# Decoder layer on one core: the feed-forward's base product in rounded halves, the normed result transposed amid the scores

## The reference

```
x = layernorm(x + mixer(x))                         # state-space mixer, 128 heads
a = softmax(x @ context^T);  x = layernorm(x + a @ context)   # per sequence, 1500 context rows
logits = x @ W_router.T;  w = normalised top 2 of softmax(logits) over 8 experts
h = x @ lora_A (8 experts x 16);  lora = (h * w) @ lora_B * 2
x = layernorm(x + x @ W_base.T + b_base + lora)
```

## Time and profile before

| | value |
|---|---|
| median of three runs | 1457.46 us |
| profiled execution, its own time | 1460.17 us |
| its span, first to last instruction | 1458.4 us |
| TensorE busy | 97% of the span |
| VectorE, ScalarE, GpSimd busy | 68%, 52%, 35% |
| mean granted TensorE clock | 0.991 of 2.4 GHz |
| chain that ended last | TensorE 89%, VectorE 6%, ScalarE 2% |
| context transfers | two of 1,024 KB to a unit, three units to a pair |

### The profile page before, as it was taken

The page is one execution under the profiler, slowest core; times in us unless marked ns, Lnnn a source line. Parts: engine busy times, 40 slices in busy tenths (PEclk is TensorE's granted clock), DMA queues, the critical chain, the costliest instruction groups (busy, mean ns, idle before and its releaser), DMA issues.

```text
span 1458.4 us, 29669 instructions
## 1 busy us (share of the span) xinstructions
PE 1418.3 (97%) x12560; PEld 1160.6 (80%) x12560; DVE 986.8 (68%) x1304; ACT 758.7 (52%) x1022; POOL 505.0 (35%) x374
## 2 busy tenths in 40 slices
PE   6999999999999999999999999999999998999996
PEld 5888989898989888988898889888888854545452
DVE  5784768476847684768476747674767496888764
ACT  6775637563746274637463646364636345543340
POOL 5252425242534153415342534243424221112101
PEclk9999999999999999999999999999999998999998
DMA  5431213121312131213121322131212177566600
GB/s 166 124 106 51 86 44 99 59 86 40 100 55 87 41 99 59 82 41 99 59 83 40 100 59 87 44 99 63 74 52 70 73 277 263 191 256 266 189 29 13
DMA packets 53405, 142.57 MB, mean 98 GB/s; under 512 B 9781, under 2 KB 9909, under 8 KB 47011
## 3 DMA queue, kind: packets, MB, share of 16 engines
q1 hardware_dynamic: 51604, 137.13, 28.9%
q0 software_dynamic: 1600, 3.44, 0.7%
q10 hardware_dynamic: 70, 0.11, 0.0%
HBM read 136.53 MB, written 2.29 MB: 95 GB/s over the span
## 4 chain that ended last, share of the span: by engine, by line
PE 89%; DVE 6%; ACT 2%; issue 1%; POOL 1%; DMA 0%; SPq 0%; DVEq 0%; POOLq 0%; ACTq 0%
PE bank L1231 45%; PE bank L1298 20%; PE bank L1539 6%; PE bank L1454 5%; PE bank L1275 4%; PE bank L1262 4%; PE bank L1511 2%; DVE conv L863 1%; PE bank L1525 1%; DVE keysT L990 1%; PE bank L1507 1%; DVE decay L922 1%; PE bank L1285 1%; PE bank L1519 1%; PE bank L1499 0%
## 5 line engine op out<-in xcount | busy, mean ns | idle before, releaser
L1231 PE MATMUL bank<-h_hi,w_hi 128*128 128x448 f32 x1152 | 337.6, 374 | 2.7 <-DVE conv L863 2.1
L437 POOL TENSOR_TENSOR y_lo<-yg,y_hi 128x896 fp32r<-128x896 f32 x63 | 134.2, 2130 | 582.4 <-ACT y_hi L621 542.4
L1231 PE MATMUL bank<-h_lo,w_hi 128*128 128x448 f32 x1152 | 327.4, 365 | 0.0
L1231 PE MATMUL bank<-h_hi,w_lo 128*128 128x448 f32 x1152 | 326.9, 365 | 0.0
L863 DVE SCALAR_TENSOR_TENSOR conv<-bank,conv_w,conv 128x880 f32<-128x880 f32 (+2 forms) x240 | 268.0, 1117 | 84.9 <-ACT conv L594 79.1
L1231 PEld LDWEIGHTS bank<-h_hi,w_lo 128*128 128x128 f32 x1152 | 216.4, 188 | 17.4
L1231 PEld LDWEIGHTS bank<-h_lo,w_hi 128*128 128x128 f32 x1152 | 216.4, 188 | 17.1
L420 POOL TENSOR_TENSOR w_lo<-w_raw,w_hi 128x512 fp32r<-128x512 f32 x144 | 186.9, 1299 | 109.5 <-ACT w_hi L561 108.1
L1231 PEld LDWEIGHTS bank<-h_hi,w_hi 128*128 128x128 f32 x1152 | 207.9, 188 | 20.7 <-DVE conv L863 2.6
L910 DVE TENSOR_TENSOR hd_dt<-bank,dt_j 128x512 f32<-128x512 f32 x128 | 82.4, 685 | 203.3 <-PE bank L1262 203.0
L1298 PE MATMUL bank<-wo_hi,y_hi 128*128 128x512 f32 x420 | 165.3, 394 | 0.0
(11 more groups left out here) (182 smaller groups left out, 1906.4 us busy)
## 6 DMA issues: line engine op xcount, KB each, us to landing
w_raw<-in_w_in SPq DMA_DIRECT2D x144, 256.0 KB, 2.9
decay<-cs_scratch SPq DMA_DIRECT2D x128, 196.0 KB
ring_a<-in_context SPq DMA_DIRECT2D x24, 1024.0 KB, 7.2
ring_b<-in_context SPq DMA_DIRECT2D x21, 1024.0 KB
wo_raw<-in_w_out SPq DMA_DIRECT2D x64, 256.0 KB, 2.7
ring_b<-in_context SPq DMA_DIRECT2D x3, 896.0 KB
acc<-in_x SPq DMA_DIRECT2D x1, 1792.0 KB, 8.9
out<-z POOLq DMA_DIRECT2D x14, 112.0 KB, 3.9
```

Source lines behind the costliest of these rows:

```text
L437: g_.tensor_tensor(y_lo[:, c % 4, :], yg[:, c % 2, :], y_hi[:, c % 4, :].bitcast(f32), ALU.subtract).then_inc(s["y_low"], 1)
L1231: last = mm(place, w[:, k * P:(k + 1) * P], x[:, k, half * HALF:(half + 1) * HALF], start=(k == 0 and i == 0), stop=(k == KT - 1 and i == 2))
```

## The change

The base product takes three of the four 128-feature blocks in rounded pieces. The weight block is split into a rounded high part `wb_hi` and the rest `wb_lo`, the data into `x2hi` and `x2lo` (type float32r), and three products (high by high, high by low, low by high) take the place of one float32 product. The fourth block stays float32 (`wb_end`). ScalarE makes `wb_hi` once at the end of round 0, GpSimd makes `wb_lo` once in round 1 (in the place of the raw weights); each pair ScalarE makes `x2hi` and VectorE `x2lo`.

The third norm works in place in `x2`, so that `z3` goes; `add_bias` now waits for the transposes of `x2`. `x1p` has two buffers instead of three, and `load_x1` runs one pair ahead instead of two.

The order changes too. `turn_x2(u-1)` stands ahead of block 12 of `score(u)`. `turn_queries` follows `turn_probs` in all rounds. VectorE transposes half 0 of all three units ahead of the three halves 1. In round 0 `last_sum(4..6)` and two sets of statistics come behind `score_max(0)`.

```diff
             def feed_forward(u):
...
                 at_least(pe, s["ffn_read"], u)
-                for k in range(KT):
-                    mm(ffn, x2T[:, k, :], wbT[:, k, :], start=(k == 0), stop=False)
+                mm(ffn, x2T[:, KT - 1, :], wb_end[:], start=True, stop=False)
+                pe.wait_ge(s["x2hi_set"], u + 1)
+                for k in range(KT - 1):
+                    mm(ffn, x2hi[:, k, :], wb_hi[:, k, :], start=False, stop=False)
+                if u == 0:
+                    pe.wait_ge(s["wb_low"], 1)
+                for k in range(KT - 1):
+                    mm(ffn, x2hi[:, k, :], wb_lo[:, k, :], start=False, stop=False)
+                pe.wait_ge(s["x2lo_set"], u + 1)
+                for k in range(KT - 1):
+                    mm(ffn, x2lo[:, k, :], wb_hi[:, k, :], start=False, stop=False)
...
             def score(u):
...
                     if b == 0:
-                        pe.wait_ge(s["kT_set"], 12 * u + 10)
+                        pe.wait_ge(s["kT_set"], 12 * u + 6)
...
+                    if b == 12:
+                        turn_x2(u - 1)
...
             def x2_evac(u):
                 act.wait_ge(s["x2_tr"], u + 1)
-                a(x2T[:], misc.rearrange("p (k t) -> p k t", k=KT), ACT.Copy).then_inc(s["x2_evac"], 1)
+                at_least(act, s["ffn_done"], u)
+                src = misc.rearrange("p (k t) -> p k t", k=KT)
+                a(x2T[:], src, ACT.Copy).then_inc(s["x2_evac"], 1)
+                act.wait_ge(s["x2_evac"], u + 1)
+                a(x2hi[:], x2T[:, 0:KT - 1, :], ACT.Copy).then_inc(s["x2hi_set"], 1)
...
+            def base_low():
+                pool.wait_ge(s["wb_high"], 1)
+                g_.tensor_tensor(wb_lo[:], wb_raw[:], wb_hi[:].bitcast(f32),
+                                 ALU.subtract).then_inc(s["wb_low"], 1)
...
+            def x2_low(u):
+
+                dve.wait_ge(s["x2_evac"], u + 1)
+                dve.wait_ge(s["x2hi_set"], u + 1)
+                at_least(dve, s["ffn_done"], u)
+                v.tensor_tensor(x2lo[:], x2T[:, 0:KT - 1, :], x2hi[:].bitcast(f32),
+                                ALU.subtract).then_inc(s["x2lo_set"], 1)
...
             for u in range(PAIRS + 1):
...
-                if following:
+                if following and u >= 1:
                     keys_part(u + 1, 0, 0)
+                    keys_part(u + 1, 1, 0)
+                if u >= 1:
+                    x2_low(u - 1)
...
                 if following:
-                    keys_part(u + 1, 0, 1)
+                    keys_part(u + 1, 2 if u >= 1 else 0, 0)
...
+                if u == 0:
+                    keys_part(1, 1, 0)
+                    keys_part(1, 2, 0)
+                    for t in range(4, TT):
+                        last_sum(t)
                 if following:
-                    keys_part(u + 1, 1, 0)
+                    keys_part(u + 1, 0, 1)
                     keys_part(u + 1, 1, 1)
...
-                    keys_part(u + 1, 2, 0)
                     keys_part(u + 1, 2, 1)
-                if u + 4 < TT:
-                    norm1_stats(u + 4)
+                if u == 0:
+                    norm1_stats(2)
+                if 0 < u <= TT - 3:
+                    norm1_stats(u + 2)
```

More of the change, by code:

```diff
@@ L144, in layer_kernel @@
         x2T = sb("x2T", [P, KT, P], f32, att)
-        wbT = sb("wbT", [P, KT, DM], f32, att)
+        x2hi = sb("x2hi", [P, KT - 1, P], f32r, att)
+        x2lo = sb("x2lo", [P, KT - 1, P], f32r, att)
+        wb_hi = sb("wb_hi", [P, KT - 1, DM], f32r, att)
+        with ExitStack() as raw:
+            wb_raw = sb("wb_raw", [P, KT - 1, DM], f32, raw)
+        wb_lo = sb("wb_lo", [P, KT - 1, DM], f32r, att)
+        wb_end = sb("wb_end", [P, DM], f32, att)
         waT = sb("waT", [P, KT, P + EXP], f32, att)
@@ L253, in x1_landed @@
         def x1_landed(u):
-            return 16 * sum(x1_pieces(k) for k in range(u % 3, u + 1, 3))
+            return 16 * sum(x1_pieces(k) for k in range(u % 2, u + 1, 2))
         def at_least(eng, semaphore, value):
@@ L739, in queries @@
                 src = turn.rearrange("p (k t) -> p k t", k=KT)
-                for c in blocks:
+                for c in range(4):
                     for row in range(4):
                         last = a(qT[SQ * row:SQ * (row + 1), :, c, :], src[SQ * c:SQ * (c + 1)], ACT.Copy)
-                if 3 in blocks:
-                    last.then_inc(s["q_set"], 1)
+                last.then_inc(s["q_set"], 1)
             def first_queries():
@@ L784, in _ @@
             first_queries()
-            for t in range(1, 4):
-                first_norm(t)
+            first_norm(1)
             for u in range(PAIRS):
@@ L1068, in _ @@
                 last_halves(t)
[L1069 to L1072, removed]
+            last_sum(1)
+            norm1_stats(1)
+            last_sum(2)
+            last_sum(3)
             steps = [1]
@@ L1500, in turn_x2, with score @@
                 last.then_inc(s["x2_tr"], 1)
+            def score(u):
+                pe.wait_ge(s["q_set"], u + 1)
+                pe.wait_ge(s["exps_done"], u)
+                pe.wait_ge(s["pT_evac0"], u)
+                pe.wait_ge(s["pT_evac12"], 2 * u)
+                for b in range(NB):
+                    if b == 0:
+                        pe.wait_ge(s["kT_set"], 12 * u + 6)
+                    elif b == NB // 2:
+                        pe.wait_ge(s["kT_set"], 12 * u + 12)
+                    if b == 12:
+                        turn_x2(u - 1)
+                    last = score_block(b)
+                    if b % 8 == 7:
+                        last.then_inc(s["s_mm"], 1)
             def feed_forward(u):
```

96 lines of the change are left out of this document (39 added, 57 removed).

## The result

The changed kernel takes 1460.21 us (median of 19 runs, 1456.95 to 1464.07) where the kernel before, run beside it, takes 1457.79 us (19 runs, 1456.45 to 1459.38). The ratio is 1.0017, 95% interval 1.0011 to 1.0024: 2.4 us slower. The forecast was 1455.4 with a range to 1460.2, so the time lies just above the range and the sign is the other one. The difference is under the 0.2% that the prediction held to be beyond measuring; with 19 runs of each kernel it stands clear of the noise.

A forecast was written before the change was run, and what follows sets the result against it. TensorE's own instructions were taken to bound the attention rounds. Gains of 3.1, 3.5 and 1.0 us minus losses of 0.2 and 5.3 made 2.1 less: 1457.46 to 1455.4 us, with an 8-in-10 range of 1449.8 to 1460.2.

The forecast's parts named there:

- round 6: Attention round 6: counted like any normal round, 0.58 us gained, with no wait for pair 7's units in the sum.
- round 0: First round: earlier row maximum gains 3.1 us at the softmax; pair 1's x1p rows arriving late cost 0.2.
- round 1: Second round: units behind the feed-forward weights make TensorE wait 2.7 us, plus slow clock; 5.3 us lost, bounds 0 and 8.
- rounds 2 to 5: Normal attention rounds: each gains 0.58 us net and takes 29.1 us, with no softmax wait exposed.
- round 7 and end: Last round: it has no turn_queries and waits 0.69 us for x2T, so it gains 1.0 us.
- Base product and transposes: TensorE in each normal round: 0.4 from the base product plus 0.35 from transposes minus 0.18, net 0.58 us gained.
- the hidden wait for x2T: Between turn_x2's transposes and the router product: the 0.25 us wait and late start go, 0.35 us gained a round.
- the break: Scores interrupted once more by turn_x2's small tiles: costs 0.18 us a round, bounds 0 and 0.5.
- Hiding the softmax: Between scores and turn_probs: 4.0 us of TensorE work covers 3.6 us of softmax; margin shrinks from 2.2 to 0.4 us.
- Rival B: Round 6: third unit lands some 17 us into the scores, about 3 us wait, 2 more to clock; 1460.5 or 1463; chance 0.12.
- rival D: Round 6: the 2.44 us TensorE stop with its slow stretch (4.6 us) goes and no unit wait comes; 1450.8 us; chance 0.08.
- The step from profile to median: Whole kernel: predicted profile 1458.1 us; the earlier profile's 2.7 us above median carried over, so 2.1 is taken off 1457.46.

The follow-up runs named there:

- e3_sums_first: Changed kernel with all seven sums ahead of the first row maximum, so the feed-forward weights load early: 1456.68 us, ratio 0.9998 to the kernel before.
- e5_sums_first_r6_later: Changed kernel with all seven sums ahead of the first maximum and, in round 6 alone, the second and third unit's parts behind the maximum: 1450.86 us, ratio 0.9942.
- e2_units_later: Changed kernel, but in rounds 1 and 6 VectorE takes the row maximum ahead of the second and third unit's parts: 1450.72 us, ratio 0.9954 to the kernel before.
- e11_changed_again: The changed kernel run again unaltered for a second profile: 1461.25 us.
- e9_x1_from_scalar: e2_units_later with pair 1's rows of x1 issued by ScalarE after its first norm, not by GpSimd: 1449.91 us, ratio 0.9947 to the kernel before.
- e10_before_third: The kernel before run again unaltered for a third profile: 1457.99 us.

## Why the prediction was wrong

The step that failed is the one on round 6: the new wait behind the third unit of pair 7 was put at nothing in the sum, and the long stop of one execution was taken for the kernel's own. The runs show 2.85 and 1.95 us of wait with the lower clock behind it, and without it round 6 is 4.8 us shorter (34.59 in e3_sums_first, 29.83 in e5_sums_first_r6_later). Means over the profiles in the table (three of before, two of the changed kernel) against the terms of the sum:

| term | predicted | measured |
|---|---|---|
| round 0 | -2.9 | -2.0 |
| round 1 (its share of 0.6 included) | +4.7 | +5.3 |
| rounds 2 to 5 | -2.3 | -1.8 |
| round 6 | -0.6 | +0.8 |
| round 7 and end | -1.0 | -1.0 |
| sum | -2.1 | +1.3 |

**Base product and transposes: right.** The best round loses 0.72 us where 0.58 was predicted. The halves save 0.50 (0.4 predicted), the hidden wait for x2T and the late starts around it 0.49 (0.35 predicted), the break costs 0.26 (0.18 predicted, within its bounds). Hiding the softmax held with its thin margin: no round from 2 to 5 waits for it. But rounds 2 to 5 gain only 1.8 us together, since not every round is like the best one; round 4, which holds a small stop, takes 30.03 and 30.08 us in the two profiles. The steps costed at nothing or beside other work came near their sizes: x2_low 0.52 us, wb_hi 1.47, wb_lo 3.48.

**Round 1: right in mechanism and near in size.** The forecast had the second unit at 1231 and a wait of 2.7 us; it was 1233 and 2.4 us with TensorE itself 1.9 us later than assumed. In the second profile TensorE starts these scores at 1219.4, as the forecast had it; there the unit comes at 1234.4, and the waits make 5.2 us. So the landing of the unit was put 2 to 3 us too early. That the moved sums caused the wait was shown by e3_sums_first.

**Round 0: mis-sized.** The gain of 3.0 us at turn_probs came as worked out. "x1p of pair 1 may land just after its transposes are due; 0.2 off" was too little: the wait was 1.9 us in the first profile, 0.8 in the second, and 0.8 to 2.8 in the other kernels with the same source of these rows.

**Round 6: the step that failed.** The sum held nothing for it. Rival B named the mechanism, its place and nearly its size (the third unit some 17 us in, a wait of about 3; it came 17.0 us in), but set it aside because "where the old stop of TensorE stays, the new wait lies under it". It did not lie under it. In the first profile the old stop is absent, which was the first half of rival D, and TensorE waits 2.85 us for the copy with the slow clock behind; in the second it has a stop of 0.89 and a wait of 1.95. The other half of the error is the scale: the stop of before was taken at 4.6 us from a single execution (34.60 against 29.69 makes 4.9), while two more show 2.3 and 3.0. Against the mean round 6 of before, 33.07, the changed one is 0.8 us longer, and without the wait it would be 3.7 us shorter (e2_units_later: 29.39).

**The step from profile to median.** "It lies 2.7 us above the median of the runs, and I take the difference to that median" treated those 2.7 us as an overhead that both kernels share. They were mostly the one slow stretch. The profiled time of the changed kernel, predicted at 1458.1, came out at 1458.29; that was luck, since round 0 gained 1.6 us less there than the sum had it and round 1 lost 1.2 us less, and the second profile took 1461.25. The median lies 1.9 us above the first profile, not 2.7 below. Read from first profile to first profile, this step is nearly the whole miss (2.7 and 1.9 of 4.8 us); read by the means, the terms are 3.4 us off. In both readings the long stop of round 6 in one execution of before has a large part.

On rival D the prediction said that the trace cannot show whether the stop is the fetch of instructions. Its transfers come close to showing it, as said above. With the new order the stop in round 6 is at most 0.99 us in eleven profiles, against 1.4 to 2.4 in three of before. The packet starts 7.9 to 8.7 us into these scores in the profiles of before, and 6.0 to 6.9 us in those of the changed kernel. What stays open is why it starts later in one execution than in another.

## What to carry to other kernels

When instructions are moved off the stretch that hid a wait, list everything that the waiting engine's queue now holds ahead of the late step, and give each transfer in it its own landing time, the worst pair's included. A few sums moved out of a stretch that had 3.5 us of slack saved VectorE nothing that mattered and delayed a load by 13 us, which came back as a wait one round further on. And one profile of each kernel is one draw: when it stands further from the median than the forecast is large, compare the stages with each other and not the totals, and ask which stage holds the excess. A wait that goes when the engine itself comes later has not been explained: look at when the transfer ran.

## What the runs showed of the hardware

The same work in round 0 takes 10.45 or 12.09 us for the value products (e11_changed_again against the first profile of the changed kernel), with starts 0.26 us apart. In e11_changed_again the twelve transposes of the probabilities already ran slow and the four of x1p at full speed again. TensorE's timeline of that run:

```profile
1204.73 2.82 PE L1564 MATMUL bank<-ident,probs 128*128 128x128 f32 x12 [3.59 <-ACT probs L786]
1208.35 0.66 PE L1373 MATMUL bank<-ident,x1p 128*128 128x128 f32 x4 [0.80 <-DMA x1p<-acc]
```

In the first profile the granted clock fell only in the course of those twelve (1.73 us) and stayed at half into the value products, as its windows show:

```profile
1204.50:1207.00 2.50, 1.73 (x12) 1.34 (x12) 2.37 (x4) 1.19 (x2) 0.00 (x0) 0.74 0.51 163
1209.00:1211.00 2.00, 2.00 (x8) 0.57 (x8) 2.00 (x4) 1.67 (x3) 0.00 (x0) 0.50 0.00 0
```

So the value products behind a wait of 3.6 us cost 1.6 us more or less by when the clock's change falls, and round 0 as a whole 2.1 (32.73 or 30.63 us), which no reading of before could tell. Small transfers (pair 1's rows of x1) took 7.7 us from issue (1200.48) to the end of TensorE's wait (1208.15); none of their packets ran in the first 3.5 us, while the context transfers held the transfer engines at a share of 1.0, and the queue of another engine made no difference (e9_x1_from_scalar). A transfer of 125 rows in one piece used about a third of the transfer engines (busy share 0.32), against 1.0 for 128 rows. And TensorE's instructions come by a queue of the same transfer engines, as far as the DMA view shows: 16 KB packets took 1.2 us in a clean case (the changed kernel, round 6) and up to 1.8 us (e10_before_third) beside context transfers, and a dense stretch of small products stopped for up to 2.4 us until 1.4 to 1.6 us after such a packet.
